# The low parts of keys and values move from DVE to Pool, and the product bank is released by the cast

## What is computed

```
q = (x @ Wq + bq).reshape(b, h, dh, t)      # b 8, h 16 heads, dh 8, t 256
k = (x @ Wk + bk).reshape(b, h, dh, t)
v = (x @ Wv + bv).reshape(b, h, dh, t)
attn = einsum('bhdt,bhds->bhts', k, v) * temperature
attn = softmax(attn, axis=-1)
out = einsum('bhdt,bhts->bhds', q, attn)
```

## Time and profile before

| | us |
|---|---|
| median of 3 runs | 489.63 (489.18 to 489.82) |
| the profiled execution | 487.31 |
| its span, first to last instruction | 485.4 |
| PE, DVE, ACT, POOL busy | 427.4, 358.5, 340.3, 262.2 |

### The profile page before, as it was taken

One profiled execution on the slowest core, in us unless ns is written; L12 is line 12 of the kernel. 1 busy time (PEld: TensorE's weight loads), 2 busy tenths in 40 slices (PEclk: granted clock), 3 DMA queues, 4 the chain that ended last, 5 costly groups with the idle time before them and its releaser, 6 DMA issues.

```text
span 485.4 us, 7696 instructions
## 1 busy us (share of the span) xinstructions
PE 427.4 (88%) x2180; PEld 286.4 (59%) x2180; DVE 358.5 (74%) x884; ACT 340.3 (70%) x902; POOL 262.2 (54%) x283
## 2 busy tenths in 40 slices
PE   3799959799799899886998889979989999799995
PEld 3577856587476577552433335324448877587783
DVE  5564884666988869769868896896748777759773
ACT  2457746798687685777998789978946566575552
POOL 2351655696776776841353454434419965656663
PEclk9999988899999999986556555555579999999999
DMA  6700003121124553643048434304115442432640
GB/s 184 220 1 1 1 1 111 65 90 43 45 95 102 150 157 87 138 101 111 2 76 108 124 80 109 88 11 96 26 24 154 127 122 80 140 108 90 174 131 22
DMA packets 45218, 43.62 MB, mean 90 GB/s; under 512 B 5500, under 2 KB 33588, under 8 KB 45176
## 3 DMA queue, kind: packets, MB, share of 16 engines
q1 hardware_dynamic: 45176, 43.13, 33.8%
HBM read 36.68 MB, written 6.43 MB: 89 GB/s over the span
## 4 chain that ended last, share of the span: by engine, by line
PE 41%; DVE 13%; issue 5%; ACT 3%; POOL 1%; POOLq 0%; DVEq 0%; ACTq 0%
PE P L1189 8%; PE P L1191 8%; PE P L1190 7%; PE P L1445 7%; PE P L1435 5%; DVE nm L866 5%; PE P L1319 1%; DVE SC L600 1%; ACT EX L1124 1%; POOL hidl L463 1%; PE P L1288 1%; PE P L1205 1%; DVE P L929 1%; PE P L1313 1%; DVE kvs L691 1%
## 5 line engine op out<-in xcount | busy, mean ns | idle before, releaser
L463 POOL TENSOR_TENSOR hidl<-tmp,hidh 128x512 fp32r<-128x512 f32 x116 | 149.3, 1295 | 83.0 <-ACT hidh L1074 82.1
L1124 ACT ACTIVATE EX<-P,nm 128x256 f32<-128x256 f32 x256 | 116.9, 499 | 14.1 <-DVE nm L866 14.0
L1074 ACT ACTIVATE hidh<-tmp 128x512 fp32r<-128x512 f32 x116 | 73.0, 630 | 48.0 <-DVE tmp L829 23.2
L866 DVE TENSOR_REDUCE nm<-P 128x4 f32<-128x1024 f32 x64 | 77.9, 1219 | 23.4 <-PE P L1435 23.1
L1445 PE MATMUL P<-EX,qs 128*32 128x256 f32 x512 | 66.8, 619 | 11.8 <-DVE O L881 11.7
L1189 PE MATMUL P<-XH,WH 128*128 128x512 f32 x176 | 75.4, 429 | 1.0 <-DVE O L881 0.5
L1191 PE MATMUL P<-XL,WH 128*128 128x512 f32 x176 | 70.1, 398 | 0.0
L1190 PE MATMUL P<-XH,WL 128*128 128x512 f32 x176 | 70.1, 398 | 0.0
L507 POOL TENSOR_TENSOR qs<-qT,rz 128x128 f32<-128x128 f32 x64 | 24.5, 404 | 79.9 <-DVE rz L874 79.9
L829 DVE TENSOR_TENSOR tmp<-P,G 128x512 f32<-128x512 f32 x64 | 43.4, 687 | 31.1 <-ACT P L1095 19.0
L1435 PEld LDWEIGHTS P<-VS,KS 24*128 24x128 f32 x256 | 30.9, 290 | 49.0 <-ACT EX L1124 34.4
(11 more groups left out here) (131 smaller groups left out, 680.9 us busy)
## 6 DMA issues: line engine op xcount, KB each, us to landing
G<-gate_rows SPq DMA_DIRECT2D x56, 256.0 KB, 3.3
kv_parts<-kvs SPq DMA_DIRECT2D x16, 256.0 KB, 2.4
VS<-kv_parts SPq DMA_DIRECT2D x48, 64.0 KB
KS<-kv_parts SPq DMA_DIRECT2D x48, 64.0 KB
G<-gate_rows SPq DMA_DIRECT2D x8, 224.0 KB, 3.0
G<-gate_rows SPq DMA_DIRECT2D x8, 192.0 KB, 3.0
G<-gate_rows SPq DMA_DIRECT2D x8, 160.0 KB, 2.6
X<-in_x SPq DMA_DIRECT2D x4, 256.0 KB, 4.6
```

The costliest lines, as they stand in the source:

```text
L463: nc.gpsimd.tensor_tensor(hidl[:, u % 3, :], source, hidh[:, u % 3, :].bitcast(fp32), ALU.subtract).then_inc(s["low_ready"], 1)
L866: v.tensor_reduce(nm1[:, g % 4, 2 * h:2 * h + 2, :], P[:, bank:bank + 2, :].rearrange("p j (h s) -> p (j h) s", h=2), AX.X, ALU.max, negat ...
L1074: sc.activation(hidh[:, u % 3, :], source, ACT.Copy).then_inc(s["high_ready"], 1)
L1124: last = sc.activation(ex1(g, j)[:, h * S:(h + 1) * S], P[:, bank_s1(g, j), h * S:(h + 1) * S], ACT.Exp, bias=nm1[:, g % 4, j, h:h + 1], a ...
```

## The change

Pool now does the subtraction that gives the low parts, in a new function low_keys(t), placed at written-out points of Pool's list: in parts 2 and 3 after its low part of steps 0, 2, 6 and 8; for tile 8 after its last expert step of the first block; for tiles 9, 10, 11 after queries(0), (1), (2); for tiles 12 to 15 after queries(11), (12), (14), (15). DVE's kv(t) ends with the cast, which counts a new semaphore kvh_ready, and no longer waits for the cast's own end. PE's claim of the bank goes by kvh_ready. SP's store still goes by kvs_ready, which Pool now counts. DVE waits, before it writes a slot of kvf again, until Pool has read it (tile t-2).

```diff
+            def low_keys(t):
+
+                pool.wait_ge(s["kvh_ready"], t + 1)
+                nc.gpsimd.tensor_tensor(kvs[:, t % KVR, 1:4:2, :], kvf[:, t % 2, :, :],
+                                        kvs[:, t % KVR, 0:4:2, :].bitcast(fp32), ALU.subtract
+                                        ).then_inc(s["kvs_ready"], 1)
+
...
                 if p + 1 < NP and i == 4:
                     low_input(0, p + 1)
+                if p >= 2 and i in (0, 2, 6, 8):
+                    low_keys(TPP * (p - 2) + (0, 2, 6, 8).index(i))
                 if p >= 1 and i == 8:
                     root(2, p - 1)
...
+            low_keys((NP - 2) * TPP)
             clear(0)
             for g in range(NG):
...
                 queries(g)
+                if g < 3:
+                    low_keys((NP - 2) * TPP + 1 + g)
+                if g in (11, 12, 14, 15):
+                    low_keys((NP - 1) * TPP + (11, 12, 14, 15).index(g))
...
+                    if t >= 2:
+                        dve.wait_ge(s["kvs_ready"], t - 1)
                     ps = P[:, bank_kv(n), (t % 2) * 2 * D:(t % 2) * 2 * D + 2 * D]
...
-                    link(v.tensor_copy(kvs[:, t % KVR, 0:4:2, :], kvf[:, t % 2, :, :]))
-                    v.tensor_tensor(kvs[:, t % KVR, 1:4:2, :], kvf[:, t % 2, :, :],
-                                    kvs[:, t % KVR, 0:4:2, :].bitcast(fp32), ALU.subtract
-                                    ).then_inc(s["kvs_ready"], 1)
+                    v.tensor_copy(kvs[:, t % KVR, 0:4:2, :], kvf[:, t % 2, :, :]).then_inc(s["kvh_ready"], 1)
...
             def project_kv(n):
-                claim(bank_kv(n), "kvs_ready", 2 * n + 2)
+                claim(bank_kv(n), "kvh_ready", 2 * n + 2)
```

More of the change, by code:

```diff
@@ L165, in two_block_adaln @@
                  "q1_ps", "q1_sb", "kv_ps",
-                 "kvs_ready", "s1_ps", "nm1_ready", "e1_ready", "rz_ready", "qs_ready", "c1_ps",
+                 "kvh_ready", "kvs_ready", "s1_ps", "nm1_ready", "e1_ready", "rz_ready", "qs_ready", "c1_ps",
                  "o1_ready", "gated", "x1_ready", "v_step", "pool_const"]
```

## The result

The changed kernel takes 495.7 us in the median of 4 executions (494.02 to 500.15) against 489.4 for the kernel before in the same set, a ratio of 1.0164 (95% interval 1.0115 to 1.0213). Measured again beside later experiments, it took 495.24 against 488.23, a ratio of 1.0153 (1.0108 to 1.0197). By medians, means and ratios the change costs 6 to 8.5 us. The prediction had the direction and, in the expert steps, the place; it was 491.5, with a range that ended at 494.0.

A forecast was written before the change was run, and what follows sets the result against it. PE was taken to lead late in the first block's expert steps, DVE where tiles 12 to 15 are made. Terms +2.8 + 0.3 - 1.5 + 0.3 = +1.9 us on 489.63 gave 491.5 us, range 487.4 to 494.0.

The forecast's parts named there:

- Pool's instruction: Each subtraction moved to Pool was taken to cost 0.7 us there, 16 of them about 11 us.
- The gate store of part 3: Expert steps, SP's queue: this store would go out at 176.4 us and not 170.15, behind the late tile stores.
- step 2 of part 3 and ahead of step 16: DVE would wait here for gate rows: 3.1 us at step 2, and 2 to 4 us ahead of step 16.
- Tiles 12 to 15: Attention: shorter DVE work on these four tiles, less waits for Pool, would give a net -1.5 us.
- The weights behind the store of tile 11: Experts' gate weights load later, the store moving from 225 to about 235 us; hidden by 1 to 2 us.
- rival 3: Slower still: low_keys on Pool makes PE wait for hidl in the expert steps; +4.1 us, 493.7 us, chance 0.13.
- kv(11): Early attention: DVE's work on tile 11 would start only after Pool's first queries, waiting until Pool has read tile 9.
- SP's store of tile 15 is 8 us late: Late attention: the store delays the loads for group 24, which have over 15 us to spare; nothing in the sum.
- the expert steps, +2.8: Late stores delay part 3's gate rows on SP's queue, so the first maximum slips 2.8 us (1.9 to 3.6).
- Row 7 of part 2: Expert steps: this gate row, behind stores 6.2 us late on SP, would still come about in time.
- tiles 9 to 11, +0.3 and +0.3: First attention groups: +0.3 us net for bank release, tiles 10 and 11; +0.3 for collisions with layer-norm statistics.
- the relief of DVE in the expert steps: DVE's saved subtractions in parts 2 and 3: at most 1.5 us, counted as nothing in the sum.

The follow-up runs named there:

- Pool late, SP's old order: Kernels with Pool's expert-step subtractions where the change put them and SP's gate-row order unchanged, among them the changed kernel: 495.7 us, 1.0164 of the kernel before.
- Pool late, gate rows first: Changed kernel with gate rows and gate store moved ahead on SP's list: 492.53 us, 1.0138; with batch 3's rows also ahead of the down weights: 489.39 us, 0.9993.
- Pool early: Changed kernel with all 16 Pool subtractions moved right behind the work that makes their input ready: 486.06 us against 488.25 for the kernel before, 0.9954.
- the stores held: Kernel before, DVE still making every low part, SP alone holding each tile's store until the changed kernel's place in Pool's list: 502.06 us against 488.63, 1.0169.

## Why the prediction was right or wrong

**Right: direction, place and sizes on Pool.** Pool's instruction took 0.738 us (0.7 said). The gate store of part 3 went out at 176.99 (176.4). DVE waited at step 2 of part 3 and ahead of step 16, where said. Tiles 12 to 15 gave 1.8 us (1.5). The weights behind the store of tile 11 came in time. PE's waits for hidl in the expert steps rose from 2.0 to 2.6 us, in other kernels with the same steps to 3.6 at most, which is less than the 2 us more that rival 3 had named; and the work on Pool, as late, is even with the kernel before once SP's list is reordered. kv(11) waited for Pool, as said.

**Wrong, the failed step: "SP's store of tile 15 is 8 us late and with it the loads for group 24; they have over 15 us".** The store was 11.6 us late and not 8, and the keys had room, as said. What the step left out is the next customer in the queue. attention_out(3) stands behind those loads and the weights, and Pool, not PE, waits for it in the middle of its list. The sum had 0 here. It cost 4.6 us in the profile after (50.8 against 46.1), 7.8 at the wait itself (queries(20) to (21)), of which 3.2 came back later. One swap of two lines took it away: 46.4 us. The prediction had followed SP's queue behind the late store as far as these loads, and stopped one entry short.

**Wrong in size: the expert steps, +2.8.** The profile after shows +2.3 there, and would seem to confirm it. That was luck. Seven profiles hold the same late placement in the expert steps and SP's old order: their keys to first maximum reach from 72.9 to 81.2 us:

```
keys to first maximum, us        profiles                                    mean
DVE makes tiles 0 to 7           70.6 71.9 70.6 71.4                         71.1
Pool late, SP's old order        72.9 74.0 75.4 76.6 79.7 80.9 81.2          77.2
Pool late, gate rows first       69.8 73.6                                   71.7
Pool early                       68.5 68.5 68.5 69.3                         68.7
```

The cost is 6.1 us in the mean. It is 3.6 in the four profiles in which the clock stayed at full, but for the last 2 us of one (72.9 to 76.6), and more in the three in which it fell to half near 190 us (79.7 to 81.2). So three terms were small. Row 7 of part 2 was called "in time" and was 3.1 us late. The gate store was given 5.3 us to land, from its rows in the kernel before, and took 6.4 to 9.3 from its issue to that of the first row. And the slow clock, in three of the seven, was not in the sum. In the Trainium skill, DMA: Bandwidth & Descriptors, "Queues, rings and completion order", each DMA engine consumes descriptors in ring order, and a DMA's semaphore increment lands only after every earlier write of that engine. The traces agree: the same four stores of attention rows landed in 2.7 us ahead of 24 loads of keys and values and in 9.3 behind them.

**Wrong in size: tiles 9 to 11, +0.3 and +0.3.** By the profiles these ten groups are 1.3 to 2.2 us longer. The wait for the slot of kvf (1.66) is the part that was named; it was set against gains that did not add up to it.

**Not seen as a gain: the relief of DVE in the expert steps.** I had counted nothing, "since what follows takes it". With the queue on time it is worth 2.4 us there (71.1 to 68.7). The Trainium skill's warning (Perfetto Trace Analysis, "Optimizing Scalar/DVE Operations") that moving work between DVE and Pool might not help did not come true here where the subtractions were early: 0.9954.

**The sum by what the runs showed.** Expert steps +3.6 (clock at full) to +6.1 (all seven), to queries(0) -0.8, first ten groups +1.7, tiles 12 to 15 -1.6, batch 3 +3.7 (means over the profiles of each kind): +6.6 to +9.1. Measured: +6.3 to +8.5 by medians and means. For Pool early the same sum gives some -5 where -2.2 was measured; the 2 to 3 us between them are not accounted for, and single profiles differ by as much in stretches that no edit touches. What also stays open is why the landing behind the same loads varies between 6.4 and 9.3 us, and what, beside the stand of PE, decides whether the clock falls.

## What to carry to other kernels

When a step moves to a less busy engine, its time there is the small part: look at which queue waits for its result, and read that queue's list to the end of what it delays, entry by entry, each with the engine that consumes it and the place in that engine's list. Put the moved step right behind the work that feeds it, and let an in-order DMA queue issue what is wanted soon (gate rows, the rows of batch 3) ahead of what is wanted late; here the same move went from 1.5% slower to 0.8% faster by the two together. And do not confirm a term by one profile when executions scatter by 2%: the one after agreed with the +2.8 for the expert steps, which seven profiles put at 6.1 in the mean.

## What the runs showed of the hardware

- A small DMA's time to land depends on what was issued ahead of it on the same queue. The four stores of attention rows took 2.7 us to land in front of the loads of keys and values and 9.3 us behind 24 of them. SP's wait for the gate store to land was 6.0 to 8.7 us in the seven profiles with Pool late and SP's old order, behind the same 12 loads as in the kernel before, where it was 5.0; why it varies is open.
- The second load of the down weights (L279) held SP for 3.6 to 8.7 us in the eleven profiles in which its group was issued within 4.5 us of the last load of keys (4.67 in the kernel after, 4.75 with Pool early); in the seven in which that was 6 us or more, as in the kernel before, the same instruction took 0.6 to 1.3 us.
- A two-input fp32 subtraction over 128x256 elements took Pool 0.718 to 0.776 us in all 16 cases, also where an instruction of DVE ran beside it, while DVE's cast of the same size spread from 0.293 to 1.102 us.
- Ahead of L1319 of part 3 (its line in the kernel after), stands of PE of 2.11, 3.20 and 3.44 us at 2.4 GHz were followed by 1.2 GHz for some 7 to 10 us; stands of 1.24, 1.30, 1.61 and 2.10 us at the same place were not. With the stores held, one of 1.86 us a few us earlier was followed by 1.2 GHz for some 3 us.
